# First stage of an attention and mixture-of-experts kernel: projections from raw x, sums by TensorE transposes, x in a ring

## The chip, the cores and the metric

One core of one Trainium2 chip. The time is the device time of one execution, in microseconds. A core has TensorE (PE in the profile; PEld are its weight loads), VectorE (DVE), ScalarE (ACT), GpSimd (POOL) and SyncE (SP), each with its own queue of instructions, and 16 DMA engines. Semaphores are the only order between engines.

## What is computed

8192 tokens of width 256, float32. The attention is over the 8 heads of one token, not over tokens:

```python
x = x + attn(layernorm(x), Wq, Wk, Wv, Wo, lambdas, ln_w, ln_b)
x = x + moe(layernorm(x), w_gate, c_fc, c_proj)

# attn, for every token
q, k, v = x @ Wq, x @ Wk, x @ Wv
q, k: (8 heads, 2 halves, 16)    v: (8 heads, 32)
a = softmax(q1 k1' / 2) v - lam * softmax(q2 k2' / 2) v   # 8 x 8 scores, twice
a = a * rsqrt(mean(a * a, over the 32 of a head) + 1e-8) * ln_w + ln_b
a = a * (1 - LAMBDA_INIT)
return a @ Wo

# moe
scores = softmax(x @ w_gate)          # 8 experts
weights, idx = top_k(scores, 2)       # a token goes to 2 experts, 1024 slots each
h = silu(x @ c_fc[e, first half]) * (x @ c_fc[e, second half])
out += weight * (h @ c_proj[e])
```

(Rotation of q and k by the position of the token leaves the scores over heads of one token as they are, so neither kernel has it.)

## The kernel before

**Stage 1** goes over 64 tiles of 128 tokens, a token per partition. **Stage 2**, the experts, goes over 16 chunks of 512 slots that a table in HBM holds; it starts when the last row of stage 1 is in the table, and the change leaves it as it is.

Each engine's program in stage 1 is a function `step(i, u, q)` that `run_tiles` calls for 16 unrolled steps, then in a loop of three turns of 16, then for 13 steps of draining. A step works on several tiles at once, each with its lag behind i; the order of the lines in `step` is the order of the engine's queue, and `past(engine, semaphore, t)` waits until a semaphore has counted tile t. A tile passes through:

- VectorE `bn_stats` (L1052) and `bn_aggr` (L1079), ScalarE `roots` (the reciprocal roots by Ln and Exp, L565 and L570), VectorE `mean_terms` (neg_mr, L917), ScalarE `normalise1` (xn, L582): the first layer norm.
- TensorE `transpose_x` (L683), ScalarE `copy_xT`, TensorE `project` (q and k, L693, 512 columns; v, L697, 256 columns). A float32 matmul is two passes in the profile, so two matmuls read x4.
- VectorE `score_products` (L869): qk_prod, 8 x 8 x 32 = 2048 products a token, one operand in PSUM; `score_sums` (L874) reduces them over 16 depths to s_raw, 128 scores; `score_max` (L879), `score_subtract` (L885), ScalarE's exponential, `prob_sum`, `prob_reciprocal`, `prob_normalise` (p_norm, L899) and `prob_difference` (w_att, L906).
- GpSimd `products` (L404): v_prod, w_att times v, 2048 products; a fold (L411) that adds two of the eight heads' blocks to two others; TensorE `sum_heads` (L705): six matmuls with the identity add the six blocks that are left.
- ScalarE `copy_a`, and `square` (L532): eight squares of 32 columns with an accumulator each; GpSimd `rms_scale` (a_n, L420); TensorE `transpose_a` (L715); ScalarE `copy_aT`; TensorE `out_project` (L724); VectorE adds to x (L861).
- `bn_stats` again (L1070, L1027), `normalise2` (rows, L586), `transpose_x2` (L732), `gate` (L745): the second layer norm and the expert logits.
- For every group of four tiles: the routing on VectorE (names with g_). g_hot (L962) marks the experts of a token; TensorE counts with a triangle matmul how many tokens stand before each (`positions`); g_over, g_slot and g_sel (L992) turn it into the slot. GpSimd `scatter` (L438) then writes the tile's rows to the slot table with two indirect DMAs, 13 tiles behind.

x lies whole in SBUF (x_all, 64 tiles), loaded by four DMAs of SP, and is stored with the attention added, eight tiles at a time. SP, after the last scatter, loads the chunks of stage 2.

GpSimd's and VectorE's orders, on which most depends, are:

```python
# GpSimd, step i: rms_scale(i - 5); products(i - 3); scatter(i - 13)
# VectorE, step i, without routing:
# score_products(i-3), bn_aggr(i-7), score_sums(i-3), score_max, mean_terms(i), score_subtract,
# bn_stats(i), attention_added(i-6), prob_sum(i-3), bn_stats(i-6), prob_reciprocal,
# bn_aggr(i), prob_normalise, prob_difference(i-3)
```

## Time and profile before

| | us |
|---|---|
| median of 3 runs | 835.03 (834.35 to 835.39) |
| profiled execution: span | 831.7 |
| TensorE busy | 722.2 (87%) |
| VectorE busy | 645.5 (78%) |
| GpSimd busy | 635.8 (76%) |
| ScalarE busy | 483.1 (58%) |
| v_prod L404, 64 of 3754 ns | 240.2 |
| qk_prod L869 and s_raw L874, 64 each | 145.9 and 145.3 |
| indirect DMAs L438, 128 of 995 ns | 127.4 |
| sum_heads L705, 768 passes | 184.0 |

The shares are over the whole span, in which stage 1 and stage 2 have different limits: over its last 230 us TensorE is busy for 215.5 us; before that see the rows below. Busy times of neighbouring instructions on one engine overlap a little in this profile, so the cost of one is read from its start to the start of the next.

### The profile page before, as it was taken

Reading aid. Unit: us, or ns where it says so; the run is one execution under the profiler, and the core shown is the slowest. Engines: PE = TensorE matmul, PEld = TensorE weight load, DVE = VectorE, ACT = ScalarE, POOL = GpSimd, SP = SyncE. Lnnn points to the kernel's source line nnn. Section 1 sums busy time; section 2 is a strip of 40 time slices with the busy share of each in tenths; the row PEclk is TensorE's granted clock in tenths of the full one; section 3 lists DMA queues with packets and bytes.
Section 4 is the critical chain, followed back from the end, with each engine's and each line's share of the span. In section 5 each row is a group of like instructions: output and inputs, shape, how many; then the busy total and the mean of one; then the engine's idle time right before and its main releaser. Section 6 shows DMA issues by size and latency. Waiting matters only on the chain.

```text
span 831.7 us, 14035 instructions
## 1 busy us (share of the span) xinstructions
PE 722.2 (87%) x3552; PEld 564.1 (68%) x3552; DVE 645.5 (78%) x1549; ACT 483.1 (58%) x1969; POOL 635.8 (76%) x419
## 2 busy tenths in 40 slices
PE   5899989998988989898898988974299999999992
PEld 2577666666765666666666666653188898989882
DVE  4899999999998999998999999954045455545540
ACT  2567766666666667665776666744155455555541
POOL 2677799898897988989799898986546668656735
PEclk8999999999999999999999999996599999999996
DMA  6994100020120121010001001001234656465524
GB/s 202 347 341 150 52 33 33 28 91 28 39 78 30 38 77 40 26 60 29 4 1 51 1 1 51 1 1 51 67 102 71 148 121 147 74 146 139 75 26 50
DMA packets 57506, 63.41 MB, mean 76 GB/s; under 512 B 7113, under 2 KB 53294, under 8 KB 57440
## 3 DMA queue, kind: packets, MB, share of 16 engines
q1 hardware_dynamic: 42080, 45.66, 17.1%
q0 software_dynamic: 15360, 17.08, 11.7%
q14 instruction: 51, 0.42, 0.2%
q8 instruction: 15, 0.25, 0.1%
HBM read 27.57 MB, written 43.78 MB: 86 GB/s over the span
## 4 chain that ended last, share of the span: by engine, by line
DVE 53%; PE 28%; issue 10%; POOL 4%; ACT 1%; DMA 1%; SPq 1%; DVEq 1%; ACTq 0%; POOLq 0%
DVE s_raw L874 16%; DVE qk_prod L869 16%; PE bank_qk L801 8%; PE bank_wo L812 4%; PE bank_v L801 4%; PE bank_a L801 4%; PE bank_g L812 4%; DVE p_norm L899 2%; DVE s_sub L885 2%; DVE p_sum L890 2%; DVE bn L1052 2%; PE bank_t L792 2%; DVE x_all L861 2%; DVE p_rec L895 2%; POOL v_prod L404 1%
## 5 line engine op out<-in xcount | busy, mean ns | idle before, releaser
L404 POOL TENSOR_TENSOR v_prod<-w_att,v_sb 128x2048 f32<-128x2048 f32 x64 | 240.2, 3754 | 55.1 <-DVE w_att L906 47.8
L705 PE MATMUL bank_a<-v_prod,ident 128*128 128x256 f32 x768 | 184.0, 389 | 31.3 <-POOL v_prod L411 31.2
L705 PEld LDWEIGHTS bank_a<-v_prod,ident 128*128 128x128 f32 x768 | 141.8, 191 | 53.4 <-POOL v_prod L411 35.9
L438 POOL DMA_INDIRECT slot_table<-rows,g_slot x128 | 127.4, 995 | 33.5 <-issue 28.0
L480 POOL DMA_INDIRECT out_dram<-y_sb,e_tok x64 | 99.4, 1553 | 65.5 <-ACT y_sb L654 51.1
L869 DVE TENSOR_TENSOR qk_prod<-bank_qk,k_sb 128x2048 f32<-128x2048 f32 x64 | 145.9, 2280 | 0.5 <-issue 0.2
L874 DVE TENSOR_REDUCE s_raw<-qk_prod 128x128 f32<-128x2048 f32 x64 | 145.3, 2271 | 0.1
L693 PE MATMUL bank_qk<-wqkv,xT 128*128 128x512 f32 x256 | 129.6, 630 | 2.7 <-ACT xT L509 1.9
L532 ACT ACTIVATE a_sq<-a_sb 128x32 f32<-128x32 f32 x512 | 109.5, 222 | 0.0
L532 ACT ACTIVATION_READ_ACCUMULATOR a_sq<-a_sb 128x1 f32 x512 | 99.3, 194 | 0.0
L411 POOL TENSOR_TENSOR v_prod<-v_prod 128x512 f32<-128x512 f32 x64 | 81.0, 1265 | 5.0
L697 PEld LDWEIGHTS bank_v<-wqkv,xT 128*128 128x128 f32 x256 | 49.5, 194 | 35.4 <-issue 32.0
L509 ACT COPY xT<-bank_t 128x256 f32<-128x256 f32 x64 | 23.8, 373 | 82.4 <-PE bank_t L683 82.3
L693 PEld LDWEIGHTS bank_qk<-wqkv,xT 128*128 128x128 f32 x256 | 44.7, 194 | 39.6 <-issue 32.1
L724 PE MATMUL bank_wo<-wo_sb,aT 128*128 128x256 f32 x256 | 67.3, 386 | 2.5 <-ACT aT L543 2.3
L697 PE MATMUL bank_v<-wqkv,xT 128*128 128x256 f32 x256 | 66.4, 382 | 0.0
L469 POOL TENSOR_TENSOR w_lo<-w,w_hi 128x1536 fp32r<-128x1536 f32 (+1 forms) x16 | 42.9, 2703 | 25.6 <-ACT w_hi L623 25.6
L645 ACT CAST h_hi<-hidden 128x512 fp32r<-128x512 f32 x48 | 29.9, 622 | 56.0 <-DVE hidden L1114 56.0
L516 ACT COPY v_sb<-bank_v 128x256 f32<-128x256 f32 x64 | 23.9, 373 | 58.0 <-POOL v_prod L411 57.9
L724 PEld LDWEIGHTS bank_wo<-wo_sb,aT 128*128 128x128 f32 x256 | 48.6, 192 | 10.4 <-ACT aT L543 4.0
L745 PEld LDWEIGHTS bank_g<-wg_sb,x2T 128*128 128x128 f32 x256 | 38.5, 197 | 24.5 <-issue 19.2
L1119 DVE TENSOR_TENSOR h_lo<-hidden,h_hi 128x512 fp32r<-128x512 f32 x48 | 33.6, 699 | 22.8 <-ACT h_hi L645 22.8
(130 smaller groups left out, 1477.7 us busy)
## 6 DMA issues: line engine op xcount, KB each, us to landing
slot_table<-fill SPq DMA_DIRECT2D x8, 1056.0 KB, 13.3
xe<-slot_table SPq DMA_DIRECT2D x16, 528.0 KB, 3.7
out_dram<-x_all SPq DMA_DIRECT2D x8, 1024.0 KB, 4.6
...
slot_table<-rows,g_slot POOLq DMA_INDIRECT x128, 2.4
...
```

Of the source, the lines that this page charges most:

```text
L404: pool.tensor_tensor(v_prod[b][:, :, :, :], w_att[b][:, :, :].rearrange("p n m -> p m n").unsqueeze(3).to_broadcast([P, H, H, DV]), v_sb[b ...
L411: pool.tensor_tensor(v_prod[b][:, 0:FOLD, :, :].rearrange("p m n e -> p (m n e)"), v_prod[b][:, 0:FOLD, :, :].rearrange("p m n e -> p (m n ...
L438: pool.indirect_dma_start(out=table, out_offset=bass.IndirectOffsetOnAxis(ap=g_slot[gb][:, j, k:k + 1], axis=0), in_=rows[:, r, :], in_off ...
L480: pool.indirect_dma_start(out=out, out_offset=bass.IndirectOffsetOnAxis(ap=e_tok[n % 2][:, k:k + 1], axis=0), in_=y_sb[n % 2][:, k, :], in ...
L532: last = nc.scalar.activation(a_sq[b][:, h, :], a_sb[b][:, h * DV:(h + 1) * DV], ACT.Square, scale=RMS_SCALE, accum_out=stat[u][:, h, 1:2])
L693: nc.tensor.matmul(bank_qk[b][:, :, :].rearrange("p a e -> p (a e)"), xT[b][:, k, :], wqkv[:, k, 0:2 * E], start=(k == 0), stop=(k == 1))
L697: last = nc.tensor.matmul(bank_v[:, 0, :], xT[b][:, k, :], wqkv[:, k, 2 * E:3 * E], start=(k == 0), stop=(k == 1))
L705: last = nc.tensor.matmul(bank_a[:, 0, :], ident[:, :], v_prod[b][:, m, :, :].rearrange("p n e -> p (n e)"), start=(m == 0), stop=(m == H ...
L724: last = nc.tensor.matmul(bank_wo[:, 0, :], aT[b][:, k, :], wo_sb[:, k, :], start=(k == 0), stop=(k == 1))
L801: last = nc.tensor.matmul(p2_h[q][half][:, :, :].rearrange("p b q -> p (b q)"), w[wb][:, k, cols], x[b][:, k, :], start=(i == 0), stop=(i ...
L869: nc.vector.tensor_tensor(qk_prod[:, :].rearrange("p (n m f) -> p n m f", n=H, m=H), q4, k4, ALU.mult).then_inc(qk_multiplied, 1)
L874: nc.vector.tensor_reduce(s_raw[b][:, :, :, :].rearrange("p n m c -> p (n m c)"), qk_prod[:, :].rearrange("p (s d) -> p s d", d=D), AX_X, ...
```

## The change

Stage 1 is rebuilt; stage 2 keeps its work.

- **Projections.** The mean over the 256 inputs is taken out of the weights at the start (`weight_means` on TensorE, `centre_weights` on VectorE), so raw x is transposed and projected. The root of the first layer norm enters as the scale of the exponential (its square, rstd_sq) and of `copy_v`. The v projection has nine more columns: the gate's eight and minus the mean.
- **Scores.** qk_prod is laid out by depth, [16, 128]. VectorE's reduction (s_part) adds the first 12 depths (D_DVE), reading in steps of 128 elements; TensorE adds the other four and s_part by transposes that accumulate in one bank (`sum_scores`, `sum_scores_part`); ScalarE copies the sum out (`copy_sT`), TensorE transposes it back, and s_max and s_sub read PSUM.
- **Heads.** Sixteen accumulating transposes (`sum_heads`) add the eight heads' blocks and leave them transposed; the fold, a_sb, the eight squares, a_n on GpSimd and transpose_a go. Mean squares over a head come from one matmul with head_ones, roots from a Ln and an Exp over 256 columns, and VectorE multiplies (`scale_a`).
- **Output and gate.** wo_aug has the nine columns too, so `out_project` gives gate logits and mean as well; ln_b enters as a row that `bias_split` cuts into three bfloat16 parts and a bfloat16 matmul adds. The squares for both layer norms are ScalarE's (`squares1`, `squares2`); bn_stats, bn_aggr, neg_mr, transpose_x2 and gate go.
- **x in a ring** of 16 tiles, loaded four at a time behind the store of the tiles that they replace.
- **Order.** GpSimd does products(i) and scatter(i - 13) only. VectorE's lags are shorter; the routing is spread over four different steps of a group.

Cut to its core (in the functions `step` the conditions that stand ahead of each call are left out):

```diff
+RING = 16
+ROWS = 8
+D_DVE = 12
+AUX = NEXP + 1
 SP
+            for g in range(NG):
+                r = g % (RING // GROUP)
+                sp.wait_ge(x1_ready, GROUP * (g + 1))
+                sp.dma_start(ov[:, g * GROUP:(g + 1) * GROUP, :], x_ring[:, r * GROUP:(r + 1) * GROUP, 0:E]).then_inc(x1_stored, 16)
+                if g + RING // GROUP < NG:
+                    sp.wait_ge(xn2_ready, GROUP * (g + 1))
+                    sp.wait_ge(x1_stored, 16 * (g + 1))
+                    load_x(g + RING // GROUP)
...
 GpSimd
             def step(i, u, q):
-                if live(i, 5):
-                    rms_scale(i - 5, (u - 5) % UNROLL, u)
-                if live(i, 3):
-                    products(i - 3, (u - 3) % UNROLL)
...
+                if live(i, 0):
+                    products(i, u % 2)
+                if live(i, SCATTER):
+                    scatter((u - SCATTER) % ROWS)
...
 TensorE
+            def sum_scores(t, b):
+                past(pe, qk_multiplied, t)
+                past(pe, ssub_ready, t, 1)
+                for d in range(D_DVE, D):
+                    nc.tensor.matmul(bank_s[:, 0, :], qk_prod[b][:, d, :], ident[:, :], is_transpose=True,
+                                     start=(d == D_DVE), stop=False, skip_group_check=True)
...
             def sum_heads(t, b):
+                past(pe, multiplied, t)
+                past(pe, an_ready, t, 2)
+                for m in range(H):
+                    for k in range(2):
+                        last = nc.tensor.matmul(bank_a[b][:, k * P:(k + 1) * P], v_prod[b][:, m, k * P:(k + 1) * P], ident[:, :],
+                                                is_transpose=True, start=(m == 0 and k == 0), stop=(m == H - 1), skip_group_check=True)
                 last.then_inc(a_summed, 1)
...
+            def out_project(t, b):
+                past(pe, an_ready, t)
...
+                nc.tensor.matmul(bank_wo[:, 0:E + AUX], ones[:, :], bias_parts[:, :], start=False, stop=True).then_inc(wo_done, 1)
...
             def step(i, u, q):
+                    project_qk(i - 1, (u - 1) % 2)
+                    sum_scores(i - 2, u % 2)
+                    sum_heads(i - 5, (u - 5) % 2)
+                    transpose_x(i, u, group_step(i, u, q, POS + 1)[0])
+                    out_project(i - 6, u % 2)
+                    sum_scores_part(i - 2, u % 2)
+                    mean_squares(i - 5, (u - 5) % 2)
+                    project_v(i - 1, (u - 1) % 2)
+                    scores_to_tokens(i - 2, u % 2)
+                    positions(g, gb, i)
...
 VectorE
+            def score_part(t, b):
+                past(dve, qk_multiplied, t)
+                past(dve, sT_done, t, 2)
+                nc.vector.tensor_reduce(s_part[b][:, :], qk_prod[b][:, 0:D_DVE, :].rearrange("p d s -> p s d"), AX_X,
+                                        ALU.add).then_inc(part_ready, 1)
...
+            def scale_a(t, b):
+                past(dve, rms_ready, t)
+                past(dve, wo_done, t, 2)
+                nc.vector.scalar_tensor_tensor(out=aT_n[b][:, :], in0=bank_a[b][:, 0:E], scalar=lnwb_s[:, 0:1], in1=aT_rms[b][:, :],
+                                               op0=ALU.mult, op1=ALU.mult).then_inc(an_ready, 1)
...
+            LOGITS, TOPS, HOTS, SLOTS_AT = 9, 11, 13, 14
...
+                    score_products(i, u % 2)
+                    score_max(i - 1, (u - 1) % 2)
+                    prob_difference(i - 2, u % 2)
+                    score_subtract(i - 1, (u - 1) % 2)
+                    slot_select(gs, bs)
+                    score_part(i, u % 2)
+                    bias_split()
+                    slot_sum(gs, bs)
+                    expert_hot(gh, bh)
+                    attention_added(i - 5, (u - 5) % RING)
```

VectorE in the step of a group that has the slot work (g_sel = slot_select). Before:

```order
L869 TENSOR_TENSOR qk_prod<-bank_qk,k_sb 128x2048 [waits scores_ready,k_copied,ln2_stats]
L982 TENSOR_TENSOR g_over<-bank_g,elimit 128x32 [waits pos_ready]
L1027 BN_AGGR stat<-bn 128x2
L874 TENSOR_REDUCE s_raw<-qk_prod 128x128 [waits qk_multiplied]
L987 SCALAR_TENSOR_TENSOR g_slot<-g_over,bank_g 128x32 [waits over_ready]
L879 TENSOR_REDUCE s_max<-s_raw 128x16 [waits scores_ready]
L992 TENSOR_TENSOR g_sel<-g_hot,g_slot 128x64 [waits slot8_ready]
```

The same step in the change:

```order
L920 TENSOR_TENSOR qk_prod<-bank_qk,k_sb 128x2048 [waits part_ready,sT_done,k_copied]
L931 TENSOR_REDUCE s_max<-bank_s 128x16 [waits scores_back]
L1042 TENSOR_TENSOR g_over<-bank_t,elimit 128x32 [waits pos_ready]
L956 SCALAR_TENSOR_TENSOR w_att<-p_norm,neg_lam 128x64 [waits multiplied,pnorm_ready]
L1047 SCALAR_TENSOR_TENSOR g_slot<-g_over,bank_t 128x32 [waits over_ready]
L937 TENSOR_TENSOR s_sub<-bank_s,s_max 128x128 [waits exp_done,smax_ready]
L1052 TENSOR_TENSOR g_sel<-g_hot,g_slot 128x64 [waits slot8_ready]
L926 TENSOR_REDUCE s_part<-qk_prod 128x128 [waits sT_done,qk_multiplied]
```

w_att moved from the end of a step to before s_sub, and g_sel from behind both long operations to between w_att and the reduction.

TensorE, a step without positions, in the change (bank_t of L694 is x; bank_a of L738 the heads; bank_s the scores):

```order
L703 MATMUL bank_qk<-wqkv,xT 128x512
L719 MATMUL bank_s<-ident,qk_prod 128x128 [waits ssub_ready,qk_multiplied]
L719 MATMUL bank_s<-ident,qk_prod 128x128 x3
L738 MATMUL bank_a<-ident,v_prod 128x128 [waits an_ready,multiplied]
L738 MATMUL bank_a<-ident,v_prod 128x128 x15
L694 MATMUL bank_t<-ident,x_ring 128x128 [waits xT_copied]
L694 MATMUL bank_t<-ident,x_ring 128x128
L752 MATMUL bank_wo<-wo_aug,aT_n 128x265 [waits x1_ready,an_ready]
L752 MATMUL bank_wo<-wo_aug,aT_n 128x265
L753 MATMUL bank_wo<-bias_parts,ones 128x265
L724 MATMUL bank_s<-ident,s_part 128x128 [waits part_ready]
```

Before, the sum of the heads came last in a step and the scores did not pass through TensorE; now out_project stands ahead of the last transpose of the scores.

GpSimd behind the last product, before:

```order
L411 TENSOR_TENSOR v_prod<-v_prod 128x512
L438 DMA slot_table<-rows,g_slot 8192x264 x2
L420 TENSOR_TENSOR a_n<-a_sb,rstd 128x256
L438 DMA slot_table<-rows,g_slot 8192x264 x2
L420 TENSOR_TENSOR a_n<-a_sb,rstd 128x256
L438 DMA slot_table<-rows,g_slot 8192x264 x18
L469 TENSOR_TENSOR w_lo<-w,w_hi 128x1536
```

and in the change:

```order
L389 TENSOR_TENSOR v_prod<-w_att,v_sb 128x2048
L407 DMA slot_table<-rows,g_slot 8192x264 x2
L228 REGISTER_ALU
L228 COMPARE_AND_BRANCH
L407 DMA slot_table<-rows,g_slot 8192x264 x26
L431 TENSOR_TENSOR w_lo<-w,w_hi 128x1536
```

The scatters of 14 tiles, 28 of them, now stand behind the last product, where 11 tiles' 22 stood.

## Rows read from the trace of the kernel before

**Rows 1.** Windows: busy us (instructions) of PE, PEld, DVE, ACT, POOL; granted clock; DMA share; GB/s
```profile
300.00:400.00 100.00, 89.52 (x412) 66.37 (x410) 96.25 (x242) 64.99 (x308) 88.51 (x60) 1.00 0.14 46
```

**Rows 2.** VectorE's timeline: start, duration, line, operation, out<-in, shapes
```profile
263.01 0.28 DVE L906 SCALAR_TENSOR_TENSOR w_att<-p_norm,neg_lam 128x64 f32<-128x64 f32 x1
...
305.29 2.28 DVE L869 TENSOR_TENSOR qk_prod<-bank_qk,k_sb 128x2048 f32<-128x2048 f32 x1
...
309.92 0.29 DVE L879 TENSOR_REDUCE s_max<-s_raw 128x16 f32<-128x128 f32 x1
310.12 0.69 DVE L917 SCALAR_TENSOR_TENSOR neg_mr<-stat,rstd 128x2 f32<-128x2 f32 x1
...
311.28 0.40 DVE L861 TENSOR_TENSOR x_all<-bank_wo,x_all 128x256 f32 x1
...
312.52 0.29 DVE L899 TENSOR_TENSOR p_norm<-probs,p_rec 128x128 f32<-128x128 f32 x1
312.85 0.52 DVE L906 SCALAR_TENSOR_TENSOR w_att<-p_norm,neg_lam 128x64 f32<-128x64 f32 x1
...
315.60 2.29 DVE L874 TENSOR_REDUCE s_raw<-qk_prod 128x128 f32<-128x2048 f32 x1
317.93 0.29 DVE L879 TENSOR_REDUCE s_max<-s_raw 128x16 f32<-128x128 f32 x1
...
339.18 2.28 DVE L869 TENSOR_TENSOR qk_prod<-bank_qk,k_sb 128x2048 f32<-128x2048 f32 x1
```

**Rows 3.** GpSimd's timeline beside it
```profile
309.54 1.26 POOL L411 TENSOR_TENSOR v_prod<-v_prod 128x512 f32<-128x512 f32 x1
310.95 1.00 POOL L438 DMA_INDIRECT slot_table<-rows,g_slot  x1 [0.15 <-issue]
312.25 0.98 POOL L438 DMA_INDIRECT slot_table<-rows,g_slot  x1 [0.30 <-issue]
```

**Rows 4.** VectorE's groups by line: busy us, mean ns of one, idle before
```profile
L885 DVE TENSOR_TENSOR s_sub<-s_raw,s_max 128x128 f32<-128x128 f32 x64 | 24.9, 389 | 0.0
...
L879 DVE TENSOR_REDUCE s_max<-s_raw 128x16 f32<-128x128 f32 x64 | 18.0, 281 | 1.3
```

**Rows 5.** TensorE's timeline, stage 1 and the first lines of a chunk
```profile
302.21 2.84 PE L705 MATMUL bank_a<-v_prod,ident 128*128 128x256 f32 x12
...
305.82 1.89 PE L693 MATMUL bank_qk<-wqkv,xT 128*128 128x512 f32 x4
307.55 1.03 PE L697 MATMUL bank_v<-wqkv,xT 128*128 128x256 f32 x4
308.41 1.03 PE L724 MATMUL bank_wo<-wo_sb,aT 128*128 128x256 f32 x4
...
640.49 1.03 PE L792 MATMUL bank_t<-ident,xe 128*128 128x128 f32 x8
```

**Rows 6.** TensorE behind its 2.68 us wait
```profile
549.73 4.30 PE L705 MATMUL bank_a<-v_prod,ident 128*128 128x256 f32 x12 [2.68 <-POOL v_prod L411]
```

**Rows 7.** The window of one us over the same place
```profile
550.00:551.00 1.00, 1.00 (x3) 0.82 (x4) 0.67 (x3) 0.80 (x2) 0.83 (x1) 0.50 0.03 8
```

**Rows 8.** VectorE at a turn of the loop
```profile
392.13 0.19 DVE L923 TENSOR_REDUCE g_max<-bank_g 128x4 f32<-128x32 f32 x1 [2.88 <-issue]
```

**Rows 9.** End of stage 1: GpSimd's last product and scatter, TensorE's first transposes
```profile
552.71 3.75 POOL L404 TENSOR_TENSOR v_prod<-w_att,v_sb 128x2048 f32<-128x2048 f32 x1
...
590.42 0.97 POOL L438 DMA_INDIRECT slot_table<-rows,g_slot  x1 [0.30 <-issue]
...
596.61 1.73 PE L792 MATMUL bank_t<-ident,xe 128*128 128x128 f32 x7 [18.87 <-DMA xe<-slot_table]
```

**Rows 10.** Start: TensorE's first projections, VectorE's products of tiles 0 and 13
```profile
7.11 3.39 PE L693 MATMUL bank_qk<-wqkv,xT 128*128 128x512 f32 x4 [0.68 <-DMA wqkv<-in_L_attn_Wv_dram]
...
14.46 2.26 DVE L869 TENSOR_TENSOR qk_prod<-bank_qk,k_sb 128x2048 f32<-128x2048 f32 x1
...
116.59 2.27 DVE L869 TENSOR_TENSOR qk_prod<-bank_qk,k_sb 128x2048 f32<-128x2048 f32 x1
```

More of the change, by code:

```diff
@@ L58, in build_block @@
     NT = NTOK // P
+    NG = NT // GROUP
     NBLK = CAP // P
@@ L111, in build_block @@
-        qk_prod = sb("qk_prod", [P, H * H * 2 * D])
-        s_raw = pair("s_raw", [P, H, H, 2])
-        s_max = pair("s_max", [P, H, 2])
-        s_sub = pair("s_sub", [P, 2, H, H])
-        probs = pair("probs", [P, 2, H, H])
-        p_sum, p_rec = pair("p_sum", [P, 2 * H]), pair("p_rec", [P, 2 * H])
-        p_norm = pair("p_norm", [P, 2, H, H])
-        w_att = pair("w_att", [P, H, H])
-        v_prod = pair("v_prod", [P, H, H, DV])
-        a_sb = pair("a_sb", [P, E])
-        a_sq = pair("a_sq", [P, H, DV])
@@ L154, in build_block @@
+        xe = [sb(f"xe{b}", [P, CB, ROW]) for b in two]
         x_hi, x_lo = ([sb(f"x_{part}{b}", [P, 2, CB * P], F32R) for b in two] for part in ("hi", "lo"))
@@ new lines, in transpose_wo, with fold_gate @@
+            def transpose_wo():
+                pe.wait_ge(wo_loaded, 16)
+                for j in range(2):
+                    for k in range(2):
+                        last = nc.tensor.transpose(bank_a[0][:, j * E + k * P:j * E + (k + 1) * P], wo_aug[:, k, j * P:(j + 1) * P], ident[:, :])
+                last.then_inc(wo_transposed, 1)
+            def fold_gate():
+                pe.wait_ge(woT_copied, 1)
+                for k in range(2):
+                    for j in range(2):
+                        last = nc.tensor.matmul(bank_a[1][:, k * AUX:(k + 1) * AUX], woT[:, j, k * P:(k + 1) * P], wqkv[:, j, 3 * E:],
+                                                start=(j == 0), stop=(j == 1))
+                last.then_inc(gate_folded, 1)
@@ new lines, in bias_row, with transpose_x @@
+            def bias_row():
+                pe.wait_ge(gate_copied, 1)
+                pe.wait_ge(lam_ready, 3)
+                for k in range(2):
+                    last = nc.tensor.matmul(bank_wo[:, 0:E + AUX], lnwb_s[:, 1:2].to_broadcast([P, P]), wo_aug[:, k, :],
+                                            start=(k == 0), stop=(k == 1))
+                last.then_inc(bias_done, 1)
+            def transpose_x(t, u, g):
+                if u % GROUP == 0:
+                    pe.wait_ge(x_loaded[u // GROUP], (t - u) + 16)
@@ L714, in transpose_a @@
                 for k in range(2):
-                    last = nc.tensor.transpose(bank_t2[:, 2 + k, :], a_n[b][:, k * P:(k + 1) * P], ident[:, :])
-                last.then_inc(an_transposed, 1)
-            def out_project(t, b):
-                if isinstance(t, int) and t == 0:
-                    pe.wait_ge(w_loaded, W_LOADS)
-                past(pe, aT_copied, t)
-                past(pe, x1_ready, t, 1)
-                for k in range(2):
-                    last = nc.tensor.matmul(bank_wo[:, 0, :], aT[b][:, k, :], wo_sb[:, k, :], start=(k == 0), stop=(k == 1))
-                last.then_inc(wo_done, 1)
@@ L1089, in _ @@
+                if ga is not None:
+                    gate_subtract(ga, ba)
             run_tiles(dve, step)
```

824 lines of the change are left out of this document (422 added, 402 removed).

## Prediction

> **What bounds the kernel now.** First the table of stretches [rows 1]: between 300 and 400 us VectorE works 96.25 us of 100, TensorE 89.52, GpSimd 88.51, ScalarE 64.99, and the granted TensorE clock is 1.00. Stage 1 is VectorE's. Second, VectorE's timeline [rows 2]: one tile is everything between two s_max rows, 309.92 to 317.93, 8.01 us; four tiles with their routing take 33.9 us (qk_prod at 305.29 to qk_prod at 339.18). Third, GpSimd's timeline over the same stretch [rows 3]: fold 1.26 us and two scatters 1.30 apart, to which come the product (3.75 at 552.71 [rows 9]) and a small a_n; GpSimd is packed nearly as tightly. Two rows read side by side carry most of what follows. neg_mr L917 works on two columns; it starts at 310.12 and ends at 310.81, and GpSimd's fold ends at 310.80. The small w_att L906 takes 0.28 us at 263.01 where GpSimd leaves it alone, 0.52 at 312.85 with a scatter running. So an operation of VectorE that reads two SBUF operands stands still while GpSimd runs a tensor operation on SBUF; the reduction s_raw, with one operand, and qk_prod, with one in PSUM, keep 2.29 and 2.28 us beside the product.
>
> **The change, engine by engine.** VectorE loses four statistics rows a tile, neg_mr, and 512 of the 2048 elements of the score reduction; it gains scale_a. Neighbours overlap by some 0.08 us, so from start to start a tile becomes: qk_prod 2.20, s_max 0.20, w_att 0.20, s_sub 0.21, s_part 2.20/2048 x 1536 = 1.65, the addition to x 0.33, p_sum 0.20, scale_a 0.33, the reciprocal 0.24, p_norm 0.20, together 5.76 us [rows 2, 4]. s_part reads its operand in steps of 512 bytes; the nearest rows are s_max, which reads in steps of 8 bytes and takes 281 ns for 128 elements, no more than the other short operations, and s_sub, which writes in such steps, and takes 389 ns against 290 of p_norm at 312.52: 0.8 ns for each element [rows 2, 4]. I take no price, as the row that only reads shows none; the upper end is 1536 x 0.8 = 1.2 us.
>
> TensorE a tile, from passes of 1.73/4 us (512 columns), 0.86/4 (256) and, for transposes of 128 columns, 1.03/8 at 640.49 [rows 5]: with 0.125 for each transpose, the projections take 1.73 + 0.89, 24 transposes 3.0, the output 0.89 + 0.12, mean squares 0.43, slots 0.08: 7.15 us, under 8.01. ScalarE works 64.99 us of 100 now, 5.5 a tile; it drops 16 short instructions a tile and gains three squares over 256 columns and a few others; even 1 us more is covered by VectorE's tile, so it is priced at nothing, and would cost its excess only over 8.3 us. GpSimd keeps product and scatters, 3.75 + 2 x 1.28 = 6.3 us; fold and a_n go. The loads of x now queue on SP behind stores, four tiles at a time, some seven tiles ahead of use; with the DMA engines 0.14 busy [rows 1] I price them at nothing; without that cover each would cost its own transfer, a few us.
>
> **The wait that is added.** GpSimd, now with slack, starts the product as soon as w_att is there: 2.7 us into VectorE's step, and it runs to 6.5. In three of four steps little stands in that window that reads two SBUF operands; but the order puts g_sel between s_sub and s_part, and g_hot behind s_part. Each has two, and each holds back everything after it on VectorE. The four steps:
> - no routing: p_norm, reached at 5.6, starts at 6.5: 6.7 us.
> - g_hot, reached at 4.45, stands to 6.5; then mask, count, sums, gate logits, partly under scatters: 9.0.
> - g_sel, reached at 3.1, stands to 6.6; then s_part and the rest: 9.9.
> - sums, maxima, indices and row writes, all with one operand: 7.7.
>
> Together 33.3 us, and 0.3 more because in the third step out_project stands on TensorE ahead of the last score transpose and waits for scale_a: 33.6, against 33.9 before. The Trainium skill ("SBUF — State Buffer", section "SBUF: two separate sides") says this pair of ports is an exclusive lock that is held for the whole instruction; the trace agrees as far as the fold goes (310.80 and 310.81), and no row shows it for L404, beside which no such operation stood. By the rule the sum stands; without it rival A's holds.
>
> **The clock.** In the g_sel step TensorE is without input for some 3.6 us. The trace has one such place: at 549.73, after 2.68 us idle, twelve passes take 4.30 us instead of 2.84, with a granted clock of 0.50 (1.2 GHz, the lower level) [rows 5 to 7]. At that price a group is 1.7 us longer. Shorter waits, which stage 1 has in plenty, leave the clock at 1.00 [rows 1]; so the cost lies between 0, should the work around the gap keep it up, and 1.7 a group; I take half, 11 us over 12.75 groups.
>
> **Start and end.** qk_prod(0), at 14.46 now [rows 10], waits also for the weight means on TensorE (3.39 + 1.03, the price of the first projections, 3.39 at 7.11 [rows 5, 10]), less their overlap with the loads, and five subtractions: 17.6. A bias split of nine dependent small operations (some 0.4 each, as 256 columns take 0.40 at 311.28 [rows 2]) puts 3.7 into step 2; the steps before the first slot work take 7.0 (two), 7.2 (seven) and 7.4 (four): 17.6 + 14.0 + 3.7 + 50.4 = 85.7 at tile 9, and 115.3 at tile 13, against 116.59 before [rows 10]. Twelve groups of 33.6, three last steps at 33.6 - 6.7 = 26.9, and two turns of the loop, in which VectorE idles 2.88 us each [rows 8], kept as they are, 5.8: 115.3 + 403.2 + 26.9 + 5.8 = 551.2, when VectorE is done with its 64 steps. At the end the last product finishes 12.0 later, since it waits for the previous product and a scatter pair. Now 22 scatters stand behind the last product (552.71), the last at 590.42, and stage 2's first transposes at 596.61 [rows 9]; in the change 28 do, 1.28 us apart: 35.8 us. They end at 599.0, 7.6 us later than 591.4. Stage 2 is as it was: 5.2 us to its first transpose and 235.1 to the end. The span: 599.0 + 5.2 + 235.1 = 839.3, with half the clock losses 850.3. The profiled span is 831.7, and the median, 835.0, lies 3.3 above it: 850.3 + 3.3 = **854**.
>
> **The rivals.**
> A, faster: the product does not hold VectorE's small operations. It decides if g_sel and g_hot last under 0.5 us beside L404. Then VectorE's step is under 7.15 on average and TensorE sets it: 85.7 us at tile 9, 55 x 7.15 + 5.8 = 399.1, the same 12.0 + 35.8 + 5.2 + 235.1 behind: 773, time 776, a floor, since every stall adds. For it: no row shows a hold by L404. Against: the fold is the same instruction on the same engine.
> B, strided reduction: s_part takes 2.85 instead of 1.65 us. It adds to the steps in which nothing held VectorE afterwards anyway, some 2.25 us a group, 29 in all: 882. Against it stands s_max; for it s_sub. The Trainium skill ("SBUF — State Buffer", "Door 1: The DMA port swizzle") says each access that crosses to a new 16-byte line pays a penalty; s_max still gets two elements of a line, s_part one, so by the rule this rival comes true, and no row here shows such a read.
> C, the clock falls oftener: in all groups at g_sel and at g_hot too, the other 11 us and, for the 9.0 us step, in which TensorE idles 1.9 us, 1.0 a group: 854 + 11 + 13 = 878. For it: 549.73. The Trainium skill ("TensorE: Matmul & The Clock Gate", "Part 4: PE-mode transpose") says transposes do not count as busy for the clock, and 24 of the new tile's instructions are transposes. If it never rose, 14.3 us a tile would give some 1150 (chance 0.03); here transposes come in twos and eights only, and no row shows twenty.
> D, little changes: shorter steps and longer tail cancel, 835.
>
> **Chances.** The forecast's mechanism 0.52, of it 0.12 below 833 (the hold binds only in part, about 820), the rest slower; A 0.18; B 0.13; C 0.12; D 0.05. Differences under 0.2% (1.7 us) can't be told from none. Faster: 0.18 + 0.12 = 0.30; same 0.05; slower 0.65. As both signs have weight: the likeliest case alone runs from 842 (clock kept) to 865 (lost in every group). The range goes from 780, just above A's floor, to 885, above B; a clock that stays low and a perfect A are left out.
>
> **What would show it.** Right: g_sel near 3.5 us and g_hot near 2, ending with a product of GpSimd; a granted clock of 0.50 once a group; s_part near 1.7; 28 scatters in a row; stage 2's first transpose at 604 to 615. Wrong: g_sel under 0.5 us (A), s_part near 2.9 (B), TensorE's busy share over 95% in stage 1 (A or C), or gaps before x's loads.

## The result, and the profile after

The changed kernel takes 891.37 us (median of 4 runs, 889.96 to 893.20) against 834.69 for the kernel before on the same chip: a ratio of 1.068, interval 1.066 to 1.070. Forecast were 854 us, 780 to 885. The direction was right; the loss is 56.7 us where 19 were forecast, and lies 6 us beyond the range. The profiled execution has a span of 889.1 us.

The windows of stage 1 after the change [rows 1]:

```profile
300.00:400.00 100.00, 80.42 (x429) 60.38 (x428) 93.80 (x177) 54.09 (x194) 61.18 (x33) 0.93 0.16 56
400.00:500.00 100.00, 82.46 (x433) 61.02 (x431) 89.08 (x180) 54.54 (x192) 60.73 (x31) 0.92 0.13 43
```

VectorE is down from 96 us of 100 to 94 and 89, TensorE from 90 to 80 and 82, GpSimd from 88 to 61; the granted clock, 1.00 before, averages 0.93. No engine is full: the engines wait for each other. VectorE's timeline over one group of four tiles [rows 2] says where:

```profile
302.40 2.28 DVE L920 TENSOR_TENSOR qk_prod<-bank_qk,k_sb 128x2048 f32<-128x2048 f32 x1
...
305.99 2.86 DVE L926 TENSOR_REDUCE s_part<-qk_prod 128x128 f32<-128x1536 f32 x1
308.76 1.03 DVE L1022 TENSOR_TENSOR g_hot<-rows,eiota 128x64 f32<-128x64 f32 x1
...
311.82 2.29 DVE L920 TENSOR_TENSOR qk_prod<-bank_qk,k_sb 128x2048 f32<-128x2048 f32 x1
...
314.81 3.78 DVE L1052 TENSOR_TENSOR g_sel<-g_hot,g_slot 128x64 f32<-128x64 f32 x1
...
322.76 2.28 DVE L920 TENSOR_TENSOR qk_prod<-bank_qk,k_sb 128x2048 f32<-128x2048 f32 x1
326.81 0.29 DVE L931 TENSOR_REDUCE s_max<-bank_s 128x16 f32<-128x128 f32 x1 [1.77 <-PE bank_s L729]
...
332.93 2.29 DVE L920 TENSOR_TENSOR qk_prod<-bank_qk,k_sb 128x2048 f32<-128x2048 f32 x1
...
339.94 2.28 DVE L920 TENSOR_TENSOR qk_prod<-bank_qk,k_sb 128x2048 f32<-128x2048 f32 x1
```

From qk_prod to qk_prod the four steps are 9.42, 10.94, 10.17 and 7.01 us: 37.5 a group, where 33.9 stood before. Two rows make them long. g_sel works on 64 columns and takes 3.78 us, from 314.81 to 318.59; and s_part takes 2.86 us for three quarters of what s_raw added up in 2.29. GpSimd's product beside g_sel:

```profile
314.76 3.74 POOL L389 TENSOR_TENSOR v_prod<-w_att,v_sb 128x2048 f32<-128x2048 f32 x1 [2.62 <-DVE w_att L956]
318.67 1.00 POOL L407 DMA_INDIRECT slot_table<-rows,g_slot  x1 [0.16 <-issue]
```

It ends at 318.50, its scatter follows at 318.67, and g_sel ends between them. g_hot, reached at 308.76, stands 1.03 us, to the end of the product before (305.95 to 309.70). The groups by line (busy us, mean ns of one, idle before [rows 4]):

```profile
L926 DVE TENSOR_REDUCE s_part<-qk_prod 128x128 f32<-128x1536 f32 x64 | 181.8, 2841 | 0.2
L920 DVE TENSOR_TENSOR qk_prod<-bank_qk,k_sb 128x2048 f32<-128x2048 f32 x64 | 146.4, 2287 | 8.5 <-issue 6.2 <-ACT k_sb L482 2.2
L1052 DVE TENSOR_TENSOR g_sel<-g_hot,g_slot 128x64 f32<-128x64 f32 x16 | 49.0, 3065 | 0.1
...
L931 DVE TENSOR_REDUCE s_max<-bank_s 128x16 f32<-128x128 f32 x64 | 18.3, 286 | 34.0 <-PE bank_s L729 34.0
...
L1022 DVE TENSOR_TENSOR g_hot<-rows,eiota 128x64 f32<-128x64 f32 x16 | 13.8, 864 | 0.0
```

s_part is 2841 ns in the mean, 64 times; s_max waits 34 us in all for TensorE, which it hardly did before (1.3). TensorE's side of the g_sel step [rows 5]:

```profile
317.97 0.38 PE L694 MATMUL bank_t<-ident,x_ring 128*128 128x128 f32 x2
322.41 1.16 PE L752 MATMUL bank_wo<-wo_aug,aT_n 128*128 128x265 f32 x4 [4.07 <-DVE aT_n L963]
...
326.35 0.42 PE L729 MATMUL bank_s<-ident,sT_sb 128*128 128x128 f32 x1
```

It is out of work at 318.35, waits 4.07 us for aT_n, and what follows is slow. The granted clock in the same place [rows 6, 7]:

```profile
320.00:322.00 2.00, 0.00 (x0) 0.00 (x0) 2.00 (x6) 0.00 (x0) 0.95 (x1) 1.00 0.37 135
324.00:325.00 1.00, 1.00 (x3) 0.75 (x3) 1.00 (x1) 0.91 (x4) 0.00 (x0) 0.50 0.00 0
327.00:328.00 1.00, 1.00 (x3) 0.38 (x2) 1.00 (x4) 0.00 (x0) 0.54 (x1) 1.00 0.00 0
```

The clock reads 1.00 from 320 to 322, while TensorE is idle, 0.50 from 324 to 325, when it works again since 322.41, and 1.00 from 327. In those microseconds lie the v projection and the transpose back of the scores (326.35), for which s_max then waits to 326.81, 1.77 us. The end of stage 1 [rows 9]:

```profile
606.73 3.75 POOL L389 TENSOR_TENSOR v_prod<-w_att,v_sb 128x2048 f32<-128x2048 f32 x1
...
647.42 0.97 POOL L407 DMA_INDIRECT slot_table<-rows,g_slot  x1 [0.30 <-issue]
...
653.63 1.09 PE L811 MATMUL bank_t<-ident,xe 128*128 128x128 f32 x4 [24.79 <-DMA xe<-slot_table]
```

The last product ends at 610.48, the last scatter at 648.40: 37.9 us. TensorE begins stage 2 at 653.63 and the span ends 235.5 later, as before.

### The profile page after: what moved, and what is told of

Read it like the earlier page. It is cut to its first block, busy times and chain, and to the rows that moved or that the text cites. A ratio compares the mean times of both kernels' runs of the same rounds, so it can differ in the third digit from the quotient of the medians.

```text
span 889.1 us, 13493 instructions
## 1 busy us (share of the span) xinstructions
PE 715.2 (80%) x3896; PEld 558.9 (63%) x3896; DVE 665.8 (75%) x1316; ACT 453.0 (51%) x1399; POOL 516.5 (58%) x296
## 4 chain that ended last, share of the span: by engine, by line
DVE 41%; PE 40%; issue 13%; POOL 2%; DMA 2%; ACT 1%; DVEq 0%; SPq 0%; POOLq 0%; ACTq 0%
DVE s_part L926 14%; PE bank_qk L820 8%; DVE g_sel L1052 5%; DVE qk_prod L920 5%; PE bank_wo L752 5%; PE bank_v L711 5%; PE bank_wo L831 4%; PE bank_v L820 4%; PE bank_a L820 4%; PE bank_a L831 4%; PE bank_a L744 2%; DVE aT_n L963 2%; DVE x_ring L968 2%; DVE s_sub L937 2%; POOL slot_table L407 1%
## 5 line engine op out<-in xcount | busy, mean ns | idle before, releaser
L926 DVE TENSOR_REDUCE s_part<-qk_prod 128x128 f32<-128x1536 f32 x64 | 181.8, 2841 | 0.2
L752 PE MATMUL bank_wo<-wo_aug,aT_n 128*128 128x265 f32 x256 | 81.8, 445 | 93.1 <-DVE aT_n L963 93.0
L407 POOL DMA_INDIRECT slot_table<-rows,g_slot x128 | 126.3, 986 | 33.6 <-issue 31.6
L738 PE MATMUL bank_a<-ident,v_prod 128*128 128x128 f32 x1024 | 125.8, 277 | 1.0 <-POOL v_prod L389 1.0
L752 PEld LDWEIGHTS bank_wo<-wo_aug,aT_n 128*128 128x128 f32 x256 | 47.3, 205 | 113.6 <-DVE aT_n L963 108.1
L738 PEld LDWEIGHTS bank_a<-ident,v_prod 128*128 128x128 f32 x1024 | 116.8, 143 | 1.5 <-POOL v_prod L389 1.5
L711 PE MATMUL bank_v<-wqkv,xT 128*128 128x265 f32 x256 | 78.9, 436 | 3.7 <-ACT v_sb L513 3.7
L719 PEld LDWEIGHTS bank_s<-ident,qk_prod 128*128 128x128 f32 x256 | 30.8, 141 | 49.6 <-issue 27.3
L1052 DVE TENSOR_TENSOR g_sel<-g_hot,g_slot 128x64 f32<-128x64 f32 x16 | 49.0, 3065 | 0.1
L719 PE MATMUL bank_s<-ident,qk_prod 128*128 128x128 f32 x256 | 38.8, 274 | 11.7 <-DVE s_sub L937 11.6
L744 PE MATMUL bank_a<-aT_sq,head_ones 128*128 128x256 f32 x128 | 44.4, 433 | 2.5 <-ACT aT_sq L528 2.5
```

The costliest lines, as they stand in the source:

```text
L407: pool.indirect_dma_start(out=table, out_offset=bass.IndirectOffsetOnAxis(ap=g_slot[gb][:, j, k:k + 1], axis=0), in_=rows[:, r, :], in_off ...
L711: last = nc.tensor.matmul(bank_v[:, 0:E + AUX], xT[b][:, k, :], wqkv[:, k, 2 * E:], start=(k == 0), stop=(k == 1))
L738: last = nc.tensor.matmul(bank_a[b][:, k * P:(k + 1) * P], v_prod[b][:, m, k * P:(k + 1) * P], ident[:, :], is_transpose=True, start=(m == ...
L752: nc.tensor.matmul(bank_wo[:, 0:E + AUX], aT_n[b][:, k * P:(k + 1) * P], wo_aug[:, k, :], start=(k == 0), stop=False)
L926: nc.vector.tensor_reduce(s_part[b][:, :], qk_prod[b][:, 0:D_DVE, :].rearrange("p d s -> p s d"), AX_X, ALU.add).then_inc(part_ready, 1)
L1052: nc.vector.tensor_tensor(g_sel[gb][:, :, :, :], g_hot[gb][:, :, :, :], g_slot8[gb][:, :, :].unsqueeze(2).to_broadcast([P, GROUP, 2, NEXP] ...
```

## The experiments

All are times of one chip in turn with the kernel before; a ratio without other words is to the kernel before. The changed kernel ran beside 834.69 us, the experiments beside 833.7 to 834.9, so a difference in us between runs of different chips is good to about 1 us. The forecast had three terms that can be taken apart: what g_sel and g_hot wait for, what the clock costs, and what the reduction costs. The theories were: the **hold** (VectorE's two-operand instructions stand while a product of GpSimd runs), the **stride** (s_part's 512-byte step, the forecast's rival B, which it had priced at nothing), the **clock** behind the gap; and against each the rival that the steps are set by TensorE or by the order of its queue.

**Stride alone: v1_contiguous.** The reduction reads as many elements, side by side. The scores are other numbers.

```diff
-nc.vector.tensor_reduce(s_part[b][:, :], qk_prod[b][:, 0:D_DVE, :].rearrange("p d s -> p s d"), AX_X,
+nc.vector.tensor_reduce(s_part[b][:, :], qk_prod[b][:, 0:D_DVE, :].rearrange("p d s -> p (d s)").rearrange("p (s d) -> p s d", d=D_DVE), AX_X,
```

> s_part reads the same 1536 elements without the step of 512 bytes (the first twelve depths are grouped in memory order instead of by depth, so the scores, and all that follows from them, are other numbers; the work is the same). Theory 'the stride is the mis-sized term': s_part falls from 2841 ns to about 1700, the slot step stays near 10 us because g_sel is still held, a group goes from 37.5 us to 34 to 35, the time to 850 to 860, near the forecast's 854. Rival 'something else in the steps is longer, the reduction costs what its 1536 elements cost': s_part stays over 2.6 us and the time at 891.

Measured: 852.55 us (850.50 to 852.84), ratio 1.021 (1.019 to 1.023): 38.8 us less than the changed kernel. By line, then the steps of a group on VectorE:

```profile
L926 DVE TENSOR_REDUCE s_part<-qk_prod 128x128 f32<-128x1536 f32 x64 | 111.4, 1740 | 0.2
...
L950 DVE TENSOR_TENSOR p_norm<-probs,p_rec 128x128 f32<-128x128 f32 x64 | 39.4, 615 | 1.9 <-issue 0.6
```

```profile
305.70 2.29 DVE L920 TENSOR_TENSOR qk_prod<-bank_qk,k_sb 128x2048 f32<-128x2048 f32 x1
...
315.04 2.29 DVE L920 TENSOR_TENSOR qk_prod<-bank_qk,k_sb 128x2048 f32<-128x2048 f32 x1
...
321.63 2.28 DVE L920 TENSOR_TENSOR qk_prod<-bank_qk,k_sb 128x2048 f32<-128x2048 f32 x1
...
326.08 2.13 DVE L1022 TENSOR_TENSOR g_hot<-rows,eiota 128x64 f32<-128x64 f32 x1
...
330.24 2.29 DVE L920 TENSOR_TENSOR qk_prod<-bank_qk,k_sb 128x2048 f32<-128x2048 f32 x1
...
333.24 3.70 DVE L1052 TENSOR_TENSOR g_sel<-g_hot,g_slot 128x64 f32<-128x64 f32 x1
...
340.13 2.28 DVE L920 TENSOR_TENSOR qk_prod<-bank_qk,k_sb 128x2048 f32<-128x2048 f32 x1
```

s_part is 1740 ns (forecast: 1.65 from start to start). The steps are 9.34, 6.59, 8.61 and 9.89 us, 34.4 a group, where the forecast had 33.6 and 0.85 for the clock. With this one term put right the forecast's group is there, and g_sel and g_hot stand 3.70 and 2.13 us. So the stride is the term that was missing; that the rest fits so well is partly luck, as the point by point account shows. s_part falls by 1101 ns, 70 us over 64 tiles, and the time by 38.8 only: VectorE is earlier at p_norm and g_hot, and both stand longer under GpSimd's product (p_norm 615 ns against 322, g_hot 1775 against 864), 33 us together.

**Hold alone: v2_moved.** g_sel, g_hot and what hangs on them stand behind p_norm, where no product runs.

```diff
                 if live(i, 1):
                     prob_normalise(i - 1, (u - 1) % 2)
+                if gs is not None:
+                    slot_select(gs, bs)
+                if gh is not None:
+                    expert_hot(gh, bh)
+                    expert_mask(gh, bh)
                 if ga is not None:
                     gate_max(ga, ba)
+                if gh is not None:
+                    expert_count(gh, bh)
+                    expert_before(gh, bh)
+                if gs is not None:
+                    slot_sum(gs, bs)
+                    slot_integer(gs, bs)
```

(and they are gone from where they stood)

> g_sel and g_hot with what hangs on them stand behind p_norm at the end of their steps, where GpSimd's product is over; the stride stays. Theory 'the hold': g_sel falls from 3.07 us to 0.2 to 0.4, g_hot from 0.86 to 0.2 to 0.4, the slot step from 10.9 to some 7.5 us, TensorE's 4 us gap and with it the fall of the clock behind it go; 6 us less a group, 891 - 75 = 816 (810 to 825). Rival 'the hold costs little, since TensorE sets the steps anyway': the time stays over 870.

Measured: 818.44 us (815.52 to 818.91), ratio 0.980 (0.977 to 0.983). By line, and g_sel in its new place:

```profile
L926 DVE TENSOR_REDUCE s_part<-qk_prod 128x128 f32<-128x1536 f32 x64 | 184.3, 2880 | 0.2
...
L950 DVE TENSOR_TENSOR p_norm<-probs,p_rec 128x128 f32<-128x128 f32 x64 | 20.4, 318 | 1.2
L931 DVE TENSOR_REDUCE s_max<-bank_s 128x16 f32<-128x128 f32 x64 | 18.2, 284 | 7.4 <-PE bank_s L729 7.2
...
323.76 0.22 DVE L1052 TENSOR_TENSOR g_sel<-g_hot,g_slot 128x64 f32<-128x64 f32 x1
```

g_sel takes 0.22 us instead of 3.78, s_max waits 7.4 us instead of 34, and with the stride still there the changed kernel is 2% faster than the one before. Where g_sel and g_hot stand, with what hangs on them, was worth 72.9 us.

**Both: v3_both.** The two edits together (the scores are other numbers).

> Both edits of the last two kernels (the scores' sums are other numbers, as in the first). If stride and hold are separate terms: VectorE's step is under 7 us, TensorE's 7.15 to 7.3 us sets it, a group takes 29 to 30 us and the time is 785 to 795. If p_norm is now held by the product (it is reached 5.6 us into the step, the product runs to 6.5), p_norm reads 0.5 to 1.2 us instead of 0.32 and the time is 795 to 810.

Measured: 784.07 us (783.69 to 785.00), ratio 0.940 (0.938 to 0.942). 38.8 and 72.9 are 111.7 apart, together 107.3: the terms are nearly independent. A window:

```profile
300.00:500.00 200.00, 188.53 (x1077) 139.18 (x1076) 186.71 (x465) 135.20 (x482) 154.54 (x81) 0.99 0.14 44
```

TensorE is 94% busy and VectorE 93%; neither share says which of them bounds stage 1 now (v9_layout_moved_14 comes back to it). p_norm reads 757 ns against 318 in v2_moved: with a short s_part VectorE reaches it while the product still runs, and p_norm has two operands in SBUF too. That is the expectation's second case, for which it had 795 to 810; the time is 11 us below that range and 1 us below the one without the hold. Whether the 4.4 us between 111.7 and 107.3 are p_norm's was not shown.

**g_sel without g_hot: v11_sel_only.** Only g_sel and the two lines behind it are moved.

```diff
+                if gs is not None:
+                    slot_select(gs, bs)
+                    slot_sum(gs, bs)
+                    slot_integer(gs, bs)
                 if ga is not None:
                     gate_max(ga, ba)
```

> The changed kernel with g_sel alone behind p_norm; g_hot stays in the product's window. g_sel held back 3.7 us in the slot step, and TensorE's long gap and the low clock behind it hung on it; g_hot held back 0.8 us. Expected: 830 to 838, that is most of the 73 us of v2_moved and g_hot the other 10 to 15. If it is 850 or more, the two stalls are not as unequal as their rows.

Measured: 826.16 us (823.56 to 831.62), ratio 0.992 (0.989 to 0.995). g_sel is 65 of the 73 us, 4 more than the expectation had at most, and g_hot 8: by the rows (3065 and 864 ns, 16 times, less the 0.2 us of their own) it would be 45 and 10. The 20 us that g_sel's part has beyond its rows are as much as the next run gives for the low clock behind its gap.

**The clock: v5_no_gap.** 32 transposes of the identity, whose result nobody reads, where TensorE idles in the g_sel step.

```diff
+                if group_step(i, u, q, POS + 1)[0] is not None:
+                    upto(pe, qk_multiplied, i, 2)
+                    for _ in range(32):
+                        nc.tensor.transpose(bank_qk[u % 2][:, 0, 0:P], ident[:, :], ident[:, :])
```

> The changed kernel with 32 transposes of the identity into a free bank (their result is not used) where TensorE otherwise idles 4 us in the slot step, so that only the clock behind the gap differs. Theory 'the gap costs the clock, 1.3 to 1.8 us a group, behind which s_max waits': the granted clock of stage 1 goes from 0.93 to 0.98 or more, s_max's waits fall by some 15 us, the time by 15 to 20, to 870 to 876. Rival 'the low clock lies beside other waits': the clock rises and the time stays within 5 us of 891.

Measured: 880.80 us (880.38 to 881.43), ratio 1.056 (1.054 to 1.058): 10.6 less than the changed kernel. TensorE's transposes in that step, two windows, and s_max:

```profile
312.44 3.66 PE L783 MATMUL bank_qk<-ident 128*128 128x128 f32 x32
...
312.00:316.00 4.00, 4.00 (x38) 3.86 (x36) 4.00 (x5) 1.77 (x8) 2.74 (x3) 1.00 0.16 58
318.00:320.00 2.00, 2.00 (x11) 1.52 (x10) 1.77 (x3) 1.60 (x6) 0.00 (x0) 1.00 0.00 0
...
L935 DVE TENSOR_REDUCE s_max<-bank_s 128x16 f32<-128x128 f32 x64 | 18.3, 287 | 10.6 <-PE bank_s L729 10.6
```

The clock stays at 1.00, s_max waits 10.6 us instead of 34, and yet the time falls by 10.6 and not by the 15 to 20 expected. The rest is lost behind the last tile, not in the groups. From tile 13's qk_prod to tile 61's the changed kernel takes 455.5 us (113.01 to 568.55) and this one 434.9 (115.54 to 550.40): 20.7 us less in 12 groups, 1.7 a group, nearly all in the step behind g_sel's. The tail gives 10.3 of it back: from the last product's end to the last scatter's it takes 48.2 us instead of 37.9, because GpSimd waits for the last group's slots:

```profile
586.20 3.75 POOL L389 TENSOR_TENSOR v_prod<-w_att,v_sb 128x2048 f32<-128x2048 f32 x1
...
616.35 0.97 POOL L407 DMA_INDIRECT slot_table<-rows,g_slot  x1 [11.18 <-ACT rows L544]
```

Ahead of it TensorE, VectorE and ScalarE all stand from 598.3 to 607.4; why, the trace does not say. So 10.6 us is not the price of the low clock; in the groups it is about 21.

And 3.66 us of nothing but transposes kept the clock up. At the end of stage 1 it even rose while 32 of them ran, from 0.50 before 616 to 1.00 from 617:

```profile
612.51 5.74 PE L783 MATMUL bank_qk<-ident 128*128 128x128 f32 x32
...
617.00:618.00 1.00, 1.00 (x12) 1.00 (x11) 0.78 (x4) 1.00 (x2) 0.33 (x1) 1.00 0.02 0
```

So the rule of the Trainium skill ("TensorE: Matmul & The Clock Gate", "Part 4: PE-mode transpose") that the prediction's rival C cites, that transposes do not count as busy for the clock, is not borne out here, for float32 transposes at least.

**TensorE's order: v4_out_later.** out_project stands behind the last score transpose, the mean squares and the v projection.

```diff
-                if live(i, 6):
-                    out_project(i - 6, u % 2)
                 if live(i, 2):
                     sum_scores_part(i - 2, u % 2)
                 if live(i, 5):
                     mean_squares(i - 5, (u - 5) % 2)
                 if live(i, 1):
                     project_v(i - 1, (u - 1) % 2)
+                if live(i, 6):
+                    out_project(i - 6, u % 2)
```

> Only TensorE's order: out_project stands behind the last score transpose, mean squares and v projection instead of ahead of them. Theory: s_max waits 34 us in all for the scores, because out_project waits for scale_a ahead of them; these waits go, 1 to 1.8 us a group, 865 to 880. Rival: the wait changes its place only (the addition to x waits for out_project, 2.4 us now), and the time stays within 5 us of 891.

Measured: 873.83 us (872.21 to 875.69), ratio 1.047 (1.044 to 1.050), 17.5 less than the changed kernel:

```profile
L931 DVE TENSOR_REDUCE s_max<-bank_s 128x16 f32<-128x128 f32 x64 | 18.3, 286 | 14.5 <-PE bank_s L729 14.3
```

s_max waits 14.5 us instead of 34. The forecast gave this order 0.3 us a group, 4 in all; it costs 1.3 a group here (439.7 us from tile 13 to tile 61 instead of 455.5). Both this run and v5_no_gap shorten one and the same wait, s_max's behind the g_sel step, so their gains must not be added. Why the order costs more than forecast, by a longer s_part or by out_project at the low clock, was not taken apart, and what it costs with the stride gone was not run.

**The stride, repaired: v7_layout.** qk_prod lies score by score again, depth innermost; TensorE's transposes now read in steps of 64 bytes, and s_sub writes in a step.

```diff
-            qk_prod = pair("qk_prod", [P, D, 2 * H * H])
+            qk_prod = pair("qk_prod", [P, 2 * H * H, D])
...
-                    nc.tensor.matmul(bank_s[:, 0, :], qk_prod[b][:, d, :], ident[:, :], is_transpose=True,
+                    nc.tensor.matmul(bank_s[:, 0, :], qk_prod[b][:, :, d], ident[:, :], is_transpose=True,
...
-                nc.vector.tensor_tensor(qk_prod[b][:, :, :].rearrange("p d (c n m) -> p (d c) n m", c=2, n=H), q4, k4,
+                nc.vector.tensor_tensor(qk_prod[b][:, :, :].rearrange("p (n m c) d -> p n m (c d)", n=H, m=H), q4, k4,
...
-                nc.vector.tensor_reduce(s_part[b][:, :], qk_prod[b][:, 0:D_DVE, :].rearrange("p d s -> p s d"), AX_X,
+                nc.vector.tensor_reduce(s_part[b][:, :], qk_prod[b][:, :, 0:D_DVE], AX_X,
```

> The changed kernel with qk_prod laid out score by score, depth innermost, as before the change: VectorE's reduction reads twelve neighbours, TensorE's four transposes read in steps of 64 bytes, s_sub writes in a step again. If TensorE's strided read is free, the time is v1_contiguous's 853 (850 to 857); if it pays as VectorE's does, the four transposes take over 1.2 us instead of 0.44 and the time is 858 to 870.

Measured: 854.40 us (853.05 to 857.89), ratio 1.025 (1.021 to 1.029). s_part 1732 ns, and TensorE's transposes of qk_prod 279 ns each against 274: its strided read costs next to nothing. s_sub, which now goes back and forth with its writes between two halves of a tile, 256 bytes apart, takes 375 ns instead of 283.

**Layout and place: v8_layout_moved.** The edits of v7_layout and v2_moved.

> That layout and g_sel and g_hot behind p_norm. This is v3_both with its sums right: 784 to 790 if TensorE's strided read is free, and, since TensorE sets the steps here (188 of 200 us busy), 64 times any excess of its transposes over 0.44 us on top otherwise: 1 us each would give 840.

Measured: 786.09 us (785.21 to 788.40), ratio 0.943 (0.940 to 0.946). TensorE's and VectorE's sums of the scores, and a window:

```profile
L719 PE MATMUL bank_s<-ident,qk_prod 128*128 128x128 f32 x256 | 42.0, 287 | 20.4 <-DVE s_sub L935 20.2
...
L924 DVE TENSOR_REDUCE s_part<-qk_prod 128x128 f32<-128x1536 f32 x64 | 110.7, 1730 | 0.1
...
300.00:400.00 100.00, 93.03 (x526) 69.60 (x524) 91.36 (x220) 66.59 (x237) 74.10 (x40) 0.98 0.16 57
```

v3_both's gain to within 2 us, with the sums as they should be.

**How many depths for whom: v6_moved_8 and v9_layout_moved_14.** The first is v2_moved with `D_DVE = 8`, the second v8_layout_moved with `D_DVE = 14`.

> v2_moved with VectorE adding 8 depths and TensorE 8 (was 12 and 4). If the strided reduction costs by the element read, 1.85 ns each, s_part falls from 2.88 to 1.95 us, and VectorE, which sets the steps, gives 0.9 us a tile, of which TensorE's four more transposes (0.44) take some back: 800 to 808. If it costs by the output (128 of them) as well, s_part stays over 2.3 us and the time at 810 to 818.

Measured: 791.66 us (789.88 to 792.30), ratio 0.949 (0.947 to 0.951).

```profile
L926 DVE TENSOR_REDUCE s_part<-qk_prod 128x128 f32<-128x1024 f32 x64 | 127.0, 1984 | 0.2 <-issue 0.2
...
400.00:500.00 100.00, 97.49 (x599) 76.34 (x597) 96.37 (x246) 69.90 (x248) 79.27 (x43) 1.00 0.10 31
```

512 elements less bring s_part from 2880 to 1984 ns, 1.75 ns for each; neighbouring ones cost 1740/1536 = 1.13 or less. The time is 8 us below the lowest expected, but the expectation's own terms, 0.9 us less and 0.44 more a tile, give 29 us off 818, which is 789: the measured 27 us agree with the terms, by chance, and the range did not follow from them. VectorE's part alone would be 57 us. Of the 30 that did not come, p_norm has 17 (577 ns instead of 318, 64 times); TensorE, 178.60 of 200 us busy in v2_moved, is 97.49 of 100 busy here; what sets the steps stands under the next run.

> v8_layout_moved with VectorE adding 14 depths instead of 12 and TensorE 2 instead of 4. Theory: TensorE sets the steps there, and p_norm, which stands half a microsecond under GpSimd's product, gives VectorE's 0.27 us more a place to hide: p_norm falls from 0.76 to some 0.5 us, TensorE loses 0.22 us a tile, the time is 770 to 778. Rival: VectorE is as much a bound as TensorE (both 92% busy), and the time is 786 or more.

Measured: 787.11 us (783.83 to 789.85), ratio 0.944 (0.940 to 0.947); v8's is 0.943: no difference. The rival's time came, but not for its reason, as neither engine's own work sets the steps.

```profile
300.00:500.00 200.00, 183.62 (x1024) 134.77 (x1022) 189.44 (x470) 135.26 (x488) 154.32 (x81) 1.00 0.14 46
```

TensorE has 184 of 200 us instead of 185 and VectorE 189 instead of 184: p_norm gave back 0.2 us (755 to 557 ns), as expected, and s_max waits 8.8 us instead of 5.5. What holds the steps is the product once more, in v8_layout_moved's step without routing:

```profile
311.68 3.75 POOL L389 TENSOR_TENSOR v_prod<-w_att,v_sb 128x2048 f32<-128x2048 f32 x1 [1.26 <-DVE w_att L955]
...
314.58 1.01 DVE L949 TENSOR_TENSOR p_norm<-probs,p_rec 128x128 f32<-128x128 f32 x1
```

The product ends at 315.43 and p_norm at 315.59, with the next qk_prod at 315.51. A product starts behind w_att, and p_norm and the next tile start behind the product: less work between the two on VectorE, or on TensorE, changes only how long p_norm stands. In v3, v6, v8 and v9 this step takes 6.59 or 6.60 us in the median and the g_sel step 7.39 or 7.40, with s_part from 1730 to 1997 ns and two, four or eight transposes on TensorE; p_norm ends 0.15 us behind the product in both, and in the sums step (7.5 to 7.6). Only in the g_hot step (7.6 to 7.7) is it free of the product. A kernel with p_norm moved out of that window was not run.

**The tail: v10_lag_12 and v12_layout_moved_lag_12.** v9 and v8 with one tile less between product and scatter.

```diff
-            LOGITS, TOPS, HOTS, SLOTS_AT = 9, 11, 13, 14
+            LOGITS, TOPS, HOTS, SLOTS_AT = 9, 11, 12, 13
...
-            POS = 15
+            POS = 14
...
-            SCATTER = 13
+            SCATTER = 12
```

> The same, with g_hot, the slots and the scatter one tile earlier (12 behind instead of 13), so that 26 scatters stand behind the last product instead of 28. Theory of the tail (scatters go one behind the other, 1.28 us each): 2.6 us less than v9_layout_moved_14. Rival: the tail's last scatters wait for the last group's slots anyway, no change; or the routing of two groups now falls into one step and gives back over 2 us.

Measured: 781.65 us (780.45 to 783.42), ratio 0.937 (0.935 to 0.939), 5.5 less than v9. Last product and last scatter:

```profile
501.06 3.75 POOL L389 TENSOR_TENSOR v_prod<-w_att,v_sb 128x2048 f32<-128x2048 f32 x1
...
538.76 0.97 POOL L407 DMA_INDIRECT slot_table<-rows,g_slot  x1 [0.30 <-issue]
```

37.7 us from the one's start to the other's, 40.7 in v9: 3.0 us, near the 2.6 of two scatters. The last product also starts 2.1 us sooner.

> v8_layout_moved (VectorE 12 depths, TensorE 4) with g_hot, slots and scatter one tile earlier. In v8's tail 44 us pass from the last product to the last scatter, 5 of them waiting for the slots of a group. One tile earlier, two scatters fewer stand there and the slots come a step sooner: 3 to 6 us less, 780 to 783. Rival: 786, if the step in which two groups' routing now meet costs TensorE or VectorE what the tail gives.

Measured: 782.02 us (778.85 to 786.92), ratio 0.938 (0.935 to 0.941). The expectation, 780 to 783, held: from the last product's end to the last scatter's 34.8 us pass instead of v8's 41.3, as two scatters and a wait of 4 us for slots are gone. It and v10_lag_12 are the fastest that ran, 6% below the kernel before and 12% below the changed one, and can't be told apart.

## Why the prediction was wrong, point by point

- **"I take no price, as the row that only reads shows none."** This is the step that failed: s_part at 1.65 us, as if its 1536 elements lay side by side. The strided read costs 2841 - 1740 = 1101 ns a tile, 0.72 ns an element, close to the upper end that the prediction had worked out from s_sub (0.8 ns, 1.2 us) and left to rival B with 0.13. It trusted s_max, whose step is 8 bytes, for a read whose step is 512. The Trainium skill ("SBUF — State Buffer", "Door 1: The DMA port swizzle") says that a 16-byte line has to be hit at least twice for full bandwidth, which draws the line between just these two, and the trace agrees for VectorE's reductions: v1_contiguous and v7_layout. The row of s_sub was misread besides: L885 writes back and forth between two halves of s_sub, 256 bytes apart, and not in steps of 8 bytes, so it was the nearer row of the two.
- **Rival B's own time, 882.** It was 9 us low. It had the price only in the steps "in which nothing held VectorE afterwards". v1 against the changed kernel shows it in all four: 0.4 us in the one without routing, 0.8 with g_hot, 1.05 with g_sel, 0.8 with the sums.
- **The clock.** The second term of wrong size, and one that the time of v1_contiguous hides. The rows' price of 1.7 us a group was right, the half that the forecast took of it was not: v5_no_gap gives 1.7 in every group, about 21 us where the forecast had 11.
- **"The product holds g_sel and g_hot."** Right, and now with a row for the product itself: g_sel 3.78 us (forecast near 3.5). 13 of the 16 g_sel and 13 of the 16 g_hot overlap a product, and each ends 0.08 or 0.09 us behind it. v2_moved: 72.9 us. The time of the likeliest case, 854, is met by the kernel without the stride, 852.55.
- **The four steps.** Forecast 6.7, 9.0, 9.9, 7.7 (no routing, g_hot, g_sel, sums), and 0.3 and 0.85 a group for out_project's place and the clock; without the stride 6.6, 8.6, 9.9, 9.3. The last is 1.6 us over its 7.7: the slow clock's work and out_project's wait come out there, as s_max's 1.71 us. The forecast had 1.15 for them, so some 0.4 us a group were missing, and the g_hot step's 0.4 too much made them up.
- **Start.** qk_prod of tile 0 at 16.04 (forecast 17.6), tile 13 at 113.0 (115.3), the bias split 4.1 us (3.7). Without the stride tile 13 comes at 109.7: the start was forecast 5.6 us too long, and the stride hides that.
- **End.** From the last product's end to the last scatter's 37.9 us (35.8): two gaps of 0.5 and 1.7 us stand in it, the first a wait for a group's slots, which the prediction had left out. Stage 2: 5.2 and 235.5 us (5.2 and 235.1).
- **Rival A** is false in its condition, since the product does hold. Its time, 776 as a floor, comes near once stride and hold are both gone: 784 to 786, TensorE 93 to 94% busy and VectorE 92 to 93%; but what sets three of the four steps there is the product's hold on p_norm, not TensorE. **Loads of x** show up nowhere in stage 1's steps.

In sum the stride, 38.8 us, is as large as all that separates forecast and measurement (891.4 - 854 = 37.4). That the rest comes out to 1.4 us is luck in part. In v1_contiguous the start is 5.6 us shorter than forecast, the time from tile 13 to the last product 3.5 longer, the tail 2.6 longer, stage 2 0.5 longer, and the median lies 1.4 above the span instead of 3.3.
